# Key tiles in pairs, maxima ahead of scores, and five moved pieces in an attention and gate kernel on one core

## What is computed

```python
xn = layernorm(x)
q, k, v = xn @ Wq, xn @ Wk, xn @ Wv
scores = (q k^T) * tril(ones)          # masked scores are 0, not minus infinity
attn = softmax(scores / sqrt(2048))    # so masked keys still weigh exp(0)
s = (attn v) @ Wo
g = silu(layernorm(xn, gamma, beta) @ ternary(Wf)^T + bias)
return x + s * g
```

## Time and profile before

| | us |
|---|---|
| median of 3 runs (lowest, highest) | 1619.94 (1616.06, 1622.37) |
| the profiled execution | 1617.84 |
| its span, first to last instruction | 1616.1 |
| projections, 0 to 396 | 396 |
| first quad, 396 to 564 | 168 |
| quads 1 to 6, each | 133 to 134 |
| last quad, 1364 to 1494 | 130 |
| output, 1494 to 1616 | 122 |

### The profile page before, as it was taken

How to read it: one execution, slowest core, us unless ns; L and a number is a source line. 1 busy time by engine, 2 the same in 40 slices (tenths; PEclk the granted TensorE clock), 3 DMA queues, 4 the chain that set the end, 5 groups by cost and what they waited for, 6 DMA issues and landing times.

```text
span 1616.1 us, 24521 instructions
## 1 busy us (share of the span) xinstructions
PE 1524.8 (94%) x8554; PEld 907.5 (56%) x8554; DVE 1052.3 (65%) x2389; ACT 775.7 (48%) x1614; POOL 868.5 (54%) x723
## 2 busy tenths in 40 slices
PE   6999999998799999999999999999999999899886
PEld 5777877786444455455544544544544554343665
DVE  7544765643687767767767776777766777650656
ACT  4333322233345565655656555665565655466110
POOL 4100000000565777877768777777776877469341
PEclk9999999999799999999999999999999999899999
DMA  6658765546931350351154146045025311211998
GB/s 202 188 179 216 237 196 183 157 157 181 215 90 34 80 145 21 82 113 56 35 114 116 35 86 145 15 98 132 23 53 119 92 35 38 89 32 55 305 343 294
DMA packets 110426, 201.42 MB, mean 125 GB/s; under 512 B 14688, under 2 KB 32736, under 8 KB 109280
## 3 DMA queue, kind: packets, MB, share of 16 engines
q1 hardware_dynamic: 99216, 177.86, 40.7%
q10 hardware_dynamic: 11088, 22.02, 4.1%
HBM read 123.22 MB, written 76.28 MB: 123 GB/s over the span
## 4 chain that ended last, share of the span: by engine, by line
PE 76%; DMA 9%; DVE 9%; SPq 2%; issue 1%; ACT 1%; POOL 1%; ACTq 0%; POOLq 0%; DVEq 0%
PE psP L1246 19%; PE psS L1316 17%; PE psO L1339 15%; PE psM L1224 14%; PE psL L1345 6%; DMA half<-mrow 3%; DMA gr<-gate 3%; DVE psM L1038 3%; DVE mx L1041 2%; PE psL L1354 2%; PE psT L1171 2%; DMA half<-k_lo 1%; SPq L546 1%; DMA rb<-r_rows 1%; ACT Pb L904 1%
## 5 line engine op out<-in xcount | busy, mean ns | idle before, releaser
L784 POOL TENSOR_TENSOR acc<-acc,Pb 128x1024 f32<-128x1024 f32 (+2 forms) x308 | 598.0, 1971 | 181.9 <-PE psO L1339 142.1
L904 ACT ACTIVATE Pb<-psS 128x512 f32<-128x512 f32 (+2 forms) x1122 | 519.6, 533 | 331.9 <-PE psS L1316 330.0
L1041 DVE TENSOR_REDUCE mx<-psM 128x1 f32<-128x512 f32 x768 | 485.8, 683 | 206.1 <-PE psM L1224 205.9
L1316 PE MATMUL psS<-half 97*128 97x512 f32 (+1 forms) x1247 | 476.9, 398 | 12.0 <-ACT Pb L904 7.4
L1224 PE MATMUL psM<-half 96*128 96x512 f32 (+3 forms) x1280 | 459.8, 387 | 29.0 <-DMA half<-k_lo 10.4
L1316 PEld LDWEIGHTS psS<-half 97*128 97x128 f32 x1247 | 235.9, 191 | 257.2 <-ACT Pb L904 99.1
L1224 PEld LDWEIGHTS psM<-half 96*128 96x128 f32 x1280 | 236.4, 192 | 108.0 <-DVE mx L1041 41.7
L1339 PE MATMUL psO<-Pb,Vs 128*32 128x512 f32 (+3 forms) x2304 | 272.5, 543 | 1.9 <-POOL Pb L767 1.9
L1038 DVE CUSTOM_DVE_ANT_0 psM<-psM,negm 128x256 f32<-128x256 f32 (+3 forms) x512 | 236.8, 518 | 51.5 <-PE psM L1224 50.7
L767 POOL TENSOR_SCALAR_AFFINE_SELECT Pb<-Pb 128x256 f32<-128x256 f32 x240 | 93.3, 405 | 112.5 <-ACT Pb L904 112.3
L727 POOL TENSOR_TENSOR rstd<-ve,mhalf 128x4 f32<-128x4 f32 x8 | 8.1, 1009 | 250.5 <-DVE ve L974 250.4
(11 more groups left out here) (101 smaller groups left out, 1472.7 us busy)
## 6 DMA issues: line engine op xcount, KB each, us to landing
half<-q_hi SPq DMA_DIRECT2D x32, 512.0 KB, 13.3
half<-k_hi SPq DMA_DIRECT2D x32, 512.0 KB, 11.2
xt<-in_L_attn_x SPq DMA_DIRECT2D x8, 1024.0 KB, 7.3
q_hi<-st_hi SPq DMA_DIRECT2D x32, 256.0 KB, 3.6
q_lo<-st_lo SPq DMA_DIRECT2D x32, 256.0 KB, 3.5
gate<-gs SPq DMA_DIRECT2D x32, 256.0 KB, 2.2
k_hi<-st_hi SPq DMA_DIRECT2D x32, 256.0 KB, 2.6
k_lo<-st_lo SPq DMA_DIRECT2D x32, 256.0 KB, 2.9
```

The costliest lines, as they stand in the source:

```text
L784: g.tensor_tensor(to[:, :, o:], to[:, :, o:], Pb[s % RING][:, heads, o:], ALU.add).then_inc(sum_done, 1)
L904: a.activation(weights(s, h)[:, o:], score_bank(s * HQ + h, last)[:, o:], ACT.Exp, scale=SCALE).then_inc(exp_done, 1)
L1041: ins = v.tensor_reduce(flat[:, heads, slots], bank[:, 0:ns * w].rearrange("p (a b c) -> p a b c", a=nh, c=w), AX.X, ALU.max)
L1316: t.matmul(score_bank(n, last)[:, o:], Ks[par][j // HALF][0:MROW + 1, h, j % HALF * P:(j % HALF + 1) * P], Qs[par][c // 2][0:MROW + 1, h, ...
```

## The change

- Every group now runs ahead(s), ahead(s+1), values(s), values(s+1).
- In `ahead` a head's maxima come before its scores, except for the last head of an odd step.
- `SHARES` spreads by an estimate of DVE's time for each bank (`COSTS`) and of each step's room (`ROOM`), not by matmul width. The split of a quad's banks becomes 75 and 65. Steps 0 and 1 of a quad go from 7 entries to 5, steps 2 and 3 from 4 to 7, steps 10 and 11 from 4 to 6, steps 22 and 23 from 4 to 7, and other steps lose as many.
- Masked keys of query chunk 0 are done in group 16 (step 32) of the quad before.
- The values of a projection chunk are turned, and summed, inside the next chunk.
- For quad 0 the high half, ones, `E`, `cum` and values are loaded before the last chunk's keys are stored; for the last quad reciprocal and Wo split move from step 4 to step 24, and with them SP's `reciprocals(0)` and `spread(0, 0)`.

```diff
-def step_time(s):
-    return width(s) + P
-OWN = NMB * sum(step_time(s) for s in range(OWN_STEPS)) // sum(step_time(s) for s in range(NSTEP))
-UPFRONT = NMB - OWN
+def step_room(s):
+    c, j = STEPS[s]
+    ahead = STEPS[(s + 2) % NSTEP]
+    scores = 1.1 + 4.4 * (CW - max(0, ahead[1] - CT * ahead[0]) * P) / CW
+    section = 1.5 * width(s) / CW
+    return scores / 2.5 + section - (1 if j == 0 else 0)
+def maxima_first(s, h):
+    return s % 2 == 0 or h < HQ - 1
+def bank_cost(bank):
+    segs = bank[0]
+    if diagonal(segs[0]):
+        return sum(0.15 + 0.47 * w / CW for _, _, _, w in segs)
+    return 0.7
+COSTS = [bank_cost(bank) for bank in MAXB]
+ROOM = [step_room(s) for s in range(NSTEP)]
+UPFRONT = min(k for k in range(NMB) if sum(COSTS[k:]) * sum(ROOM) <= sum(COSTS) * sum(ROOM[:OWN_STEPS]))
+def masked_keys(qn, gr):
+    found = [(qn, c) for c in range(NCH) if gr == FIRST[c] + (c > 0) and (c or qn == 0)]
+    if gr == FIRST[NCH - 1] + 4 and qn + 1 < NQUAD:
+        found.append((qn + 1, 0))
+    return found
 def max_order(banks):
...
         steps = [(s, h) for s in range(first, end) for h in range(HQ)]
-        whole, past, k = sum(step_time(s) for s, _ in steps), 0, start
+        costs = [COSTS[e[2]] if e[0] == "bank" else 0.4 for e in order[start:upto]]
+        whole, cost, past, spent, k = sum(ROOM[s] for s, _ in steps), sum(costs), 0, 0, start
         for s, h in steps:
-            past += step_time(s)
-            to = start + (upto - start) * past // whole
+            past += ROOM[s]
+            to = k
+            while to < upto and (spent + costs[to - start] / 2) * whole < cost * past:
+                spent += costs[to - start]
+                to += 1
+            if (s, h) == steps[-1]:
+                to = upto
...
                 for j in range(CT):
                     sp.wait_ge(gs_done, START + n * CT + j + 1)
                     sp.dma_start(gate_t[n * CT + j], gs[j % 2][:]).then_inc(gs_out[j % 2], 16)
+                if n == NCHUNK - 1:
+                    sp.wait_ge(P_full, START + n * NPU + AT_GATE + CT)
+                    load_half(0, 0, 1)
+                    load_ones(0, 1)
+                    load_chunk(0, 0)
+                    load_values(0, 0)
                 for k in range(NQ, 2 * NQ):
                     store_parts(k)
                 if n == EARLY_CHUNKS[0] - 1:
...
                 if n == NCHUNK - 3:
                     store_maxima(0, 0)
                 if n == NCHUNK - 1:
                     store_maxima(0, 1)
-                    sp.wait_ge(P_full, START + n * NPU + AT_GATE + CT)
-                    load_chunk(0, 0)
-                    load_values(0, 0)
-                    load_half(0, 0, 1)
-                    load_ones(0, 1)
                     load_chunk(0, 1)
                 sp.wait_ge(vs_done, (n + 1) * CT)
                 for m in range(NQ):
...
                 store_maxima(qn, 2)
                 load_chunk(qn, 2)
                 if not more:
-                    reciprocals(0)
                     for i in range(2):
                         sp.wait_ge(ost_out[i], START + NQ * NCH // 2 * 16)
                         sp.dma_start(ac[i][:], numerators(0, i)).then_inc(ac_in[i], 16)
...
                 load_chunk(qn, 3)
                 if more:
                     store_maxima(qn + 1, 0)
-                else:
-                    spread(0, 0)
                 store_chunk(qn, 2)
                 if more:
                     load_chunk(qn + 1, 0)
                     store_maxima(qn + 1, 1)
                 else:
+                    reciprocals(0)
+                    spread(0, 0)
                     sp.wait_ge(wo_done, 2)
                     spread(0, 1)
                 if qn + 2 < NQUAD:
...
+                def later_keys(qn, c):
+                    i, k = c % 2, qn * NCH + c
+                    pool.wait_ge(NE_done, START + k).then_inc(pool_waited, 1)
+                    g.iota(later[:], pattern=[[-1, CW]], base=T - 1 - c * CW, channel_multiplier=0,
+                           allow_small_or_imprecise_dtypes=True).then_inc(later_done, 1)
+                    pool.wait_ge(sub_done, START + k + 1)
+                    pool.wait_ge(E_done, START + k + 1)
+                    g.tensor_tensor(cum[i][:], cum[i][:], E[i][:], ALU.mult).then_inc(SE_done, 1)
+                    pool.wait_ge(SE_done, START + k + 1)
+                    pool.wait_ge(later_done, START + k + 1)
+                    g.tensor_tensor(E[i][:], later[:], E[i][:], ALU.mult).then_inc(NE_done, 1)
                 for gr, (c, j) in enumerate(GROUPS):
                     s = 2 * gr
                     if on_diagonal(s):
...
-                    if gr == FIRST[c] + (c > 0):
...
+                    for masked in masked_keys(qn, gr):
+                        later_keys(*masked)
             quads(quad)
...
                 for h in range(HQ):
+                    beside = max_share(qn, s - 2, h) if s >= 2 else []
+                    if maxima_first(s, h):
+                        max_rows(beside)
                     act.wait_ge(S_full, (qn * NSTEP + s) * HQ + h + 1)
                     a.activation(weights(s, h)[:, o:], score_bank(s * HQ + h, last)[:, o:], ACT.Exp, scale=SCALE).then_inc(exp_done, 1)
-                    if s >= 2:
-                        max_rows(max_share(qn, s - 2, h))
+                    if not maxima_first(s, h):
+                        max_rows(beside)
             exps(0, 0)
+            def exp_masked(qn, c):
+                i = c % 2
+                act.wait_ge(e_in[i], (qn * (NCH // 2) + c // 2 + 1) * HQ * 16)
+                a.activation(E[i][:], E[i][:], ACT.Exp, scale=SCALE).then_inc(E_done, 1)
+                act.wait_ge(cum_in[i], (qn * (NCH // 2) + c // 2 + 1) * 16)
+                if c == 0:
+                    act.wait_ge(tot_in, (qn + 1) * 16)
+                a.activation(cum[i][:], cum[i][:], ACT.Identity, bias=tot[:, 0:1], scale=-1.0).then_inc(sub_done, 1)
             def quad(qn, par, more, follows):
                 for gr, (c, j) in enumerate(GROUPS):
                     exps(qn, 2 * gr + 1, not more)
-                    if gr == FIRST[c] + (c > 0):
...
+                    for masked in masked_keys(qn, gr):
...
                     if gr + 1 < NG:
                         exps(qn, 2 * gr + 2, not more)
                     elif more:
...
                 if ahead:
                     moments(n + 1)
                 low(0)
+                if n:
+                    sums(n - 1)
                 low(1)
                 if ahead:
                     normal(n + 1)
...
+            def sums(n):
+                c = n % NCH
...
                     v.tensor_copy(carry[:, m:m + 1], cs[m][:, CW - 1:CW]).then_inc(carry_done, 1)
             chunks(chunk)
+            sums(NCHUNK - 1)
             def reciprocals(b):
                 dve.wait_ge(lr_in, (b + 1) * 16)
...
                             maxima(max_share(qn, s, h))
                     if j == 0 and (c > 0 or follows):
                         denominators(*((qn, c - 1) if c else (qn - 1, NCH - 1)))
-                        if c == 1 and not more:
+                        if c == NCH - 1 and not more:
                             reciprocals(0)
                             dve.wait_ge(wo_in, 16)
...
                 for m in range(NQ):
                     cols = slice(m * P, (m + 1) * P)
-                    pe.wait_ge(vs_done, (n - 1) * CT + m + 1) if n else pe.wait_ge(xl_done, KT)
+                    pe.wait_ge(xl_done, (n + 1) * KT)
+                    if n:
+                        pe.wait_ge(vs_done, (n - 1) * CT + m + 1)
                     if n == 0 and m == NQ - 1:
                         pe.wait_ge(wprep, 1)
                     product(m, [(part(w_hi[0], cols), part(X)), (part(w_hi[0], cols), part(XL)), (part(w_lo[0], cols), part(X))], 0)
                     early(n, early_slot("queries", m))
+                    if n and m == 0:
+                        turn_values(n - 1)
                 if n == 0:
                     gate_weights()
                 pe.wait_ge(yl_done, START + (n + 1) * KT)
...
                     pe.wait_ge(lo_done, n * 2 * NQ + NQ + j + 1)
                     cols = slice(j * P, (j + 1) * P)
                     product(j, [(part(X, cols), part(w_hi[2])), (part(XL, cols), part(w_hi[2])), (part(X, cols), part(w_lo[2]))], 2)
+            def turn_values(n):
                 pe.wait_ge(vs_done, (n + 1) * CT)
                 for m in range(NQ):
                     if m < 2:
...
                     transposes(psT[m], vs, m, V_full)
             chunks(chunk)
+            turn_values(NCHUNK - 1)
             pe.wait_ge(vs_done, NCHUNK * CT)
...
                 def run(s, ahead, slots):
                     for h in range(HQ):
+                        beside = max_share(qn, slots, h) if slots is not None else []
+                        if slots is None or maxima_first(slots, h):
```

(10 more changed lines are left out.)

18 lines of the change are left out of this document (1 added, 17 removed).

## The result

The changed kernel takes 1596.4 us (1594.55 to 1598.25) where the kernel before takes 1621.06 in four runs (1616.06 to 1622.37): a ratio of 0.9853, 95% interval 0.9829 to 0.9878. It is faster, by a third of what was forecast and outside the range. The profiled execution took 1595.97 us, its span is 1594.2.

What follows compares the result with a forecast made beforehand. PE was taken to bound full groups, with waits at the boundary and a DMA behind it, and DMA the output. Gains of 39.0 (quads 1 to 6), 19.7 (quad 0), 8.3 (last quad) and 4.6 (projections) gave 1548 us, range 1532 to 1575.

Steps and rivals of the forecast that it cites:

- Pairs: Full groups of quads 1 to 6: fewer changes between wide and 32-column matmuls gain 3.1 us a quad, bounds 0 and 3.7.
- the stretch to step 12: From the boundary to step 12, ended by a DMA: no gain from pairs or spreading, the boundary's gain is kept.
- with 5 us to spare: Chunk 3 of a quad: POOL's adds and two masks make 34.3 of 40 us, so POOL stays hidden.
- about nothing: Paired section: PE's wait for DVE's reductions before the eighth maxima matmul, 3.5 against 3.6 us, is put at nothing.
- 1.4 + 1.1 + 0.9: Gains in us per quad, quads 1 to 6: boundary block 1.4, clock behind it 1.1, spreading 0.9.
- Spreading: Quads 1 to 6: maxima moved to ACT-paced diagonal sections shorten full sections behind step 12; 0.9 us a quad, bounds 0 and 2.
- 11.5 go: Start of quad 0: earlier loads land near 394 and remove 11.5 us of waiting before the first maxima.
- The second rival: Early loads land no earlier, or hold up the last keys' stores and step 4's maxima row: 1560 us, chance 0.1.
- Last quad: Sum for the last quad: -7.9 - 2.0 + 3.4 - 1.8 = -8.3 us, bounds -4 and -12.
- the stand: Last quad: PE stands 7.9 us while DVE's reciprocal and Wo split run in front of the maxima; forecast to go.
- Projections: Turning a chunk's values behind the next chunk's first product saves 0.66 x 7 chunks = 4.6 us, bounds 2 and 5.
- The first rival: Pairs and clock give nothing: DVE or ACT runs dry in the longer values stretch, dips stay; 1578 us, chance 0.15.

Runs made afterwards that it cites:

- The runs with half adds: POOL's adds over the first half of the queries only, in the changed kernel (1572.68 us) and in that kernel with its pairs undone (1572.04 us).
- the run that has it back: Changed kernel with pairs undone, and the last quad's reciprocal, Wo split and values of step 24 in their old places: 1588.28 us, 0.9801.
- the kernel with the rows ahead: Changed kernel with pairs undone, and in every quad the maxima row of chunk 2 issued ahead of the next quad's 4 MB: 1560.40 us, 0.9628.

## Why the prediction was right and wrong

**Pairs: the step was wrong in sign.** The forecast counted TensorE's changes between wide and narrow matmuls (3.1 us a quad) and checked DVE and ACT. It did not cost the move of `values(s)` by a whole section for those who wait for the values. POOL's adds at a chunk's start are among them. For the stretch to step 12 the forecast had POOL's work "about equal" to the DMA's time and didn't ask when it starts, though it has a due point inside: the masks before the diagonal values of step 8. In chunk 3 it had left POOL hidden "with 5 us to spare", by a sum without the masked keys, of 3 us each and there twice now; in the changed kernel POOL works there without a break from 771.41 to 806.7. Measured, 18.7 us lost in all, 18.6 forecast as won in quads 1 to 6 alone. The runs with half adds and with unpaired first groups show it for the changed kernel. That the saving itself is empty is the second part: with quick adds the pairs give nothing. A paired section near the short end and its values take 4.20 + 2.71 = 6.91 us, where the earlier trace rows have 6.98 for a group, 0.07 less instead of 0.31. The values give their part of it (2.71 us, before 1.85 + 1.00). The section doesn't: by the 3.76 us of its matmuls and 0.19 for one change it would take 3.95, and the rest of its 4.2 is waiting. In the section shown, PE's sixth and seventh maxima matmul start 0.52 and 0.59 behind the one before instead of 0.47, each 0.1 behind the end of a DVE reduction (0.61 us each from 734.05 on). The forecast had put this wait at "about nothing"; it had looked at the eighth matmul alone. How DVE and ACT divide that rest isn't told apart.

**Quads 1 to 6 without the pairs** came out as forecast: without pairs they sum to 780.2 us, 18.5 less than before; 3.4 a quad (1.4 + 1.1 + 0.9) made 20.4. What was wrong is how it was divided. Spreading is not 0.9 us of full sections made shorter: behind the start of step 12's scores the kernel without pairs takes 98.2 to 100.2 us, and 97.5 before. Its gain is half of the boundary, since fewer narrow maxima stand in the block of steps 0 and 1, and only with both the waits for ACT and those for DVE gone did the clock stay up at all seven boundaries.

**The stretch to step 12** came out right by luck. The forecast took 25.9 us, the longest of the six quads before (24.9 to 25.9), as set by the DMA. The 25.97 us of the changed kernel are set by POOL's masks, and without pairs it is 24.3.

**Quad 0: the step "11.5 go" was wrong** in what is late next. The forecast named the sums and ACT's first exps. The loads did what was forecast (the first maxima start 10.9 us earlier in the quad). What came late was the row of maxima for step 12, queued behind 7 MB for quad 1. The second rival had such a loss in it, but by another way: its row is the one for step 4, behind the last keys' stores, and TensorE didn't wait for that row; nor did its other condition hold, that the loads land no earlier. Undoing the early loads costs 2.2 us instead of 12.5, and moving quad 1's loads behind the row gives 7.5. Pairs gave +1.5 there (165.6 against 164.1) instead of -2.2; the new spreading gave 5.4 (169.5 against 164.1, both without pairs) instead of 2.5.

**Last quad:** -7.8 against -8.3, right in total by luck, as errors cancelled. The moves alone gave 11.1 (129.3 to 118.2), against 6.5 in the forecast. POOL's adds were slowed by 3.0 (forecast 2.4). But the stand was 9.4 us in the run that has it back, not 7.9, and POOL's chain of adds began 12.5 us earlier in the quad (76.7 and 89.2 us after its start), not 9.9 less 1.0. The pairs cost 4.6 (122.8 and 118.2), where 1.8 was forecast as won.

**Projections:** -6.0 against -4.6, above the bound of 5 by one. The term itself is right: TensorE's waits for the copies before the turning fall from 5.4 us to 0.7. The rest may be spread, for the kernel before with pairs alone, whose projections are the old ones, reaches quad 0 at 394.3 instead of 396.4; the early first loads are not in it, since the kernel with late ones reaches quad 0 at 389.5 too.

**Output:** +2.4 against 0. This isn't the change: the profiled runs of all seventeen kernels, with the same code there, took 121.2 to 124.7 us for it, so it is spread between runs.

**The range.** The first rival, pairs and clock give nothing, gave 1578, and the kernel without pairs took 1577.7; but the clock and boundary did give their part there, and quad 0 didn't. The bounds for the pairs were 0 and 3.7 although nothing in the rows excluded a loss. The 3.3 us a quad that they cost alone, in place of 3.1 won, would have moved 1548 by 6 x 6.4 = 38 to 1586.

## What to carry to other kernels

When two pieces of work on the bounding engine are put together, write down for each piece that moves later who waits for its semaphore, and follow that engine to its next due point, not to its sum over the stage; here, the old order in each chunk's first full group alone gave back 17.1 of 18.7 us. When a load is moved ahead in a queue, look for the small transfer that stands behind the large ones not needed yet. Edits that meet at one place, here two waits in a block whose length goes with the clock behind it, are to be costed together, since each can be worth nothing alone.

## What the runs showed of the hardware

- **Clock.** The block of narrow matmuls at the boundary was followed by a granted clock of 0.59 when PE was busy for 4.57 of 5.60 us of it, and by 1.00 when it was busy for 3.88 of 4.20. Values and row sums take 4.2 us in the first case and 2.5 in the second, so a block 1.4 us longer costs 3.1. It is no rule: behind a block of 5.56 us with 4.52 busy the clock stayed at 1.00, and in the kernel with the rows ahead, behind one of seven boundaries, a block of 4.36 us with 4.04 busy was followed by 0.62.
- **A small row behind large loads** on the same queue: the row issued by 437.07 landed at 446.6, with 7 MB issued from 409.45 to 418.63 ahead of it. In the kernel without pairs, where TensorE's wait for it was 6.4 us, it was gone with 4 MB of them moved behind the row.
- **Beside DVE's split of 4.37 us** with two SBUF inputs, four POOL adds took 12.45 us instead of 9.42. The Trainium skill, "SBUF — State Buffer", section "SBUF: two separate sides", has the two lock each other out for the whole instruction, and gives the port to whichever starts first. The trace agrees only in part: POOL lost 3.0 of the 4.4 us, more than on the product in the earlier trace rows and still less than the full length, and the third add, which started 1.2 us ahead of the split (1432.88 and 1434.04), still took 3.38 us instead of 2.39.
- **A change between 512-column matmuls with 128 and with 32 weight columns** costs 0.31 us there and back by the starts in the earlier trace rows, where nothing else is waited for. Of twelve fewer a quad the timelines show 0.14 us each in the values (2.71 us instead of 1.85 + 1.00), and the time of the kernel nothing that the runs can tell.
